# A decoder layer on one core: cross attention with one score pass, transposed exponentials and other PSUM banks

## What is computed

```python
Q = (q @ W_q.T + b_q).reshape(b, -1, NH, HD).transpose(0, 2, 1, 3)   # q: layernorm(x); NH = 16, HD = 32
K = (k @ W_k.T + b_k).reshape(b, -1, NH, HD).transpose(0, 2, 1, 3)   # k = v = context
V = (v @ W_v.T + b_v).reshape(b, -1, NH, HD).transpose(0, 2, 1, 3)
scores = jnp.einsum('bhqd,bhkd->bhqk', Q, K) / math.sqrt(HD)
scores = jnp.where(causal, -jnp.inf, scores)
scores = jnp.where(padding_mask[:, None, None, :], -jnp.inf, scores)
attn = jax.nn.softmax(scores, axis=-1)
out = jnp.einsum('bhqk,bhkd->bhqd', attn, V)
return out.transpose(0, 2, 1, 3).reshape(b, -1, H) @ W_o.T + b_o
```

## Time and profile before

| what | value |
|---|---|
| median of 3 runs | 4943.44 us (4933.94 to 4956.82) |
| the profiled execution, its own time | 4941.54 us |
| its span, first to last instruction | 4939.4 us |
| granted PE clock over the span | 0.919 |
| PE, DVE, ACT, POOL busy | 88%, 62%, 30%, 21% |

### The profile page before, as it was taken

The page is one execution under the profiler, slowest core; times in us unless marked ns, Lnnn a source line. Parts: engine busy times, 40 slices in busy tenths (PEclk is TensorE's granted clock), DMA queues, the critical chain, the costliest instruction groups (busy, mean ns, idle before and its releaser), DMA issues. The chain is left out here.

```text
span 4939.4 us, 62871 instructions
## 1 busy us (share of the span) xinstructions
PE 4366.1 (88%) x23000; PEld 2976.2 (60%) x23000; DVE 3085.8 (62%) x6572; ACT 1487.3 (30%) x2991; POOL 1046.1 (21%) x631
## 2 busy tenths in 40 slices
PE   7999999987989898986789779779888969999999
PEld 5667677755666666663544444454364447777777
DVE  5888888854888888886543344245234356666664
ACT  3433343323333333331134124214213411111111
POOL 1333333330444444444000000100100000000000
PEclk8999999998999999998877988889888879999999
DMA  2011111002111111111321321232132130000000
GB/s 97 35 38 36 37 38 38 33 15 87 36 46 40 40 36 46 40 37 53 129 78 33 119 82 48 96 101 60 57 116 68 39 105 26 31 30 26 30 26 22
DMA packets 146922, 265.55 MB, mean 54 GB/s; under 512 B 27188, under 2 KB 33336, under 8 KB 146616
## 3 DMA queue, kind: packets, MB, share of 16 engines
q1 hardware_dynamic: 144568, 261.27, 16.0%
q10 hardware_dynamic: 2048, 0.27, 0.0%
HBM read 164.58 MB, written 88.08 MB: 51 GB/s over the span
## 5 line engine op out<-in xcount | busy, mean ns | idle before, releaser
L1721 DVE TENSOR_REDUCE xa_mx<-xa_s 128x1 f32<-128x1024 f32 (+7 forms) x512 | 371.4, 746 | 343.7 <-PE xa_s L1795 336.1
L1623 ACT ACTIVATE xa_src<-xa_gen 128x512 f32<-128x512 f32 (+3 forms) x768 | 357.4, 491 | 547.4 <-PE xa_gen L1815 396.5
L1812 PE MATMUL xa_gen<-xa_qa,xa_ka 98*128 98x512 f32 (+3 forms) x768 | 351.6, 487 | 84.0 <-ACT xa_src L1623 52.4
L72 PE MATMUL ff_wb<-ff_w_hi,ff_st_hi 128*128 128x512 f32 x768 | 322.8, 420 | 17.1 <-DVE ff_parts L2308 11.1
L1572 POOL TENSOR_TENSOR xa_kq<-xa_kq 128x512 f32<-128x512 f32 x32 | 40.8, 1274 | 1374.8 <-DVE xa_kq L1727 1374.8
L1794 PE MATMUL xa_s<-xa_ka,xa_qa 97*128 97x512 f32 (+3 forms) x768 | 255.1, 398 | 78.5 <-DVE xa_mx L1721 55.8
L1812 PEld LDWEIGHTS xa_gen<-xa_qa,xa_ka 98*128 98x128 f32 x768 | 167.9, 222 | 251.0 <-issue 121.8
L73 PE MATMUL ff_wb<-ff_w_hi,ff_st_lo 128*128 128x512 f32 x768 | 310.2, 404 | 0.0
L74 PE MATMUL ff_wb<-ff_w_lo,ff_st_hi 128*128 128x512 f32 x768 | 309.4, 403 | 0.0
L1203 PE MATMUL mb_ib<-mb_wc,mb_yT 128*128 128x512 f32 x512 | 268.0, 672 | 1.8 <-DVE mb_y L974 1.0
L1203 PE MATMUL mf_ib<-mf_wc,mf_yT 128*128 128x512 f32 x512 | 249.6, 633 | 1.8 <-DVE mf_y L974 1.0
(11 more groups left out here) (513 smaller groups left out, 11395.6 us busy)
## 6 DMA issues: line engine op xcount, KB each, us to landing
xa_qa<-xa_q_dram SPq DMA_DIRECT2D x384, 64.0 KB, 2.0
xa_ka<-xa_k_dram SPq DMA_DIRECT2D x384, 64.0 KB, 2.0
xa_q_dram<-xa_kq SPq DMA_DIRECT2D x32, 512.0 KB, 2.8
xa_k_dram<-xa_kq SPq DMA_DIRECT2D x32, 512.0 KB, 2.8
mf_xg<-in_x_dram SPq DMA_DIRECT2D x16, 512.0 KB, 5.2
turned_dram<-mf_xt_hi SPq DMA_DIRECT2D x16, 512.0 KB, 2.6
turned_dram<-mf_xt_lo SPq DMA_DIRECT2D x16, 512.0 KB, 4.0
part_dram<-mf_hb SPq DMA_DIRECT2D x32, 256.0 KB, 2.0
```

Of the source, the lines that this page charges most:

```text
L72: nc.tensor.matmul(out, w_hi, x_hi, start=first, stop=False)
L1623: a_.activation(pe_x[:, s % 2, hh, 0:w], gen["p2", g, s, hh][:, 0:w], ACT.Exp, scale=XSCALE)\
L1721: v_.tensor_reduce(mx[:, g % 2, i, hh:hh + 1], s1[g, hh, i][:, 0:(i + 1) * P], AX.X, ALU.max)\
L1812: last = mm(ps[:, 0:n], ka[sl][0:ROW_MAX + 1, j * P:(j + 1) * P], qa[sl][0:ROW_MAX + 1, a:a + n], start=True, stop=not diagonal)
```

## The change

Scores are made once, with queries on the partitions. `W_q` and `b_q` are multiplied by `-XSCALE`, so the scores come negated and DVE takes a minimum (L1749), which is then the bias of the exponential: ACT computes `exp(-s + min)` from the same PSUM tile, up to 1024 columns wide, with the row sums in its accumulator (`accum_out`). PE transposes the exponentials in blocks of 128x128, up to four to a bank (`packs`, L1848), ACT and DVE copy the packs in turn to `pT`, and `weigh` uses them (L1864), now 128 queries at a time. The matmuls with ones, the second score pass, the row of maxima with its copies and DMAs are gone. DVE takes one reciprocal of 16 columns for a half, PE spreads it over partitions (`spread`, L1873), DVE copies that and multiplies. `gen` has three banks, the score tensors are handed out as four single banks or two pairs (`ScoreBanks`), `acc` has one. `ka` of slots 4 to 7 lies in `st_hi`, so group 1 is loaded when the projections are done. The order is one step for each query tile: the transposes and the weighing of the tile before stand between the four scores of this one.

```diff
+def packs(i):
+    if i == 0:
+        return [[(hh, 0) for hh in range(HG)]]
+    if i == 1:
+        return [[(hh, j) for hh in (a, a + 1) for j in range(2)] for a in (0, 2)]
+    out = []
     for hh in range(HG):
+        for a in range(0, i + 1, QT):
+            out.append([(hh, j) for j in range(a, min(i + 1, a + QT))])
     return out
...
+    def by_vector(i, k):
+        return k % 2 == 1 or i == 0
...
+        def loads(g):
+            for half in range(2):
+                for h in range(g * HG, (g + 1) * HG):
+                    yield "load", (h, "q", half)
+                    yield "load", (h, "k", half)
...
+            for n in range(len(TILES) + 1):
+                now, last = TILES[n] if n < len(TILES) else None, TILES[n - 1] if n else None
...
+                if scale:
+                    yield "scale", scale.pop()
+                yield from turns(0)
+                yield from turns(1)
+                yield from one("score", 0)
+                yield from turns(2)
+                yield from one("exp", 0)
+                yield from one("score", 1)
+                yield from turns(3)
+                yield from one("exp", 1)
+                yield from one("score", 2)
+                for _ in range(2):
+                    if todo and n > 0:
+                        yield todo.pop(0)
+                done = last and last[1] % QT == QT - 1
+                if done:
+                    yield "recip", (last[0], last[1] // QT)
+                if last:
+                    yield "av", last
+                if done:
+                    yield "spread", (last[0], last[1] // QT)
+                    scale.append((last[0], last[1] // QT))
+                yield from one("exp", 2)
+                yield from one("score", 3)
+                yield from one("exp", 3)
+                if now and now[1] == NT - 1 and now[0] + 2 < NHG:
+                    yield from loads(now[0] + 2)
+                if not todo and n == 4:
+                    yield from loads(1)
+                if now and now[0] == NHG - 1 and now[1] > QT + 1:
+                    yield "o", now[1] - QT - 2
...
-        gen = Banks(ctx, nc, tag + "gen", 2, gen)
-        s1 = Banks(ctx, nc, tag + "s1", 2, s1, 2 * BANK)
-        acc = Banks(ctx, nc, tag + "acc", 2, acc)
+        gen = Banks(ctx, nc, tag + "gen", 3, gen)
+        s1 = ScoreBanks(ctx, nc, tag + "s1", s1)
+        acc = Banks(ctx, nc, tag + "acc", 1, acc)
...
+                    a_.activation(pq[:, hh, 0:w], s1[g, i, hh][:, 0:w], ACT.Exp, scale=-1.0, bias=mn[:, i % 2, hh:hh + 1],
+                                  accum_out=sums[:, i // QT, i % QT, hh:hh + 1]).then_inc(p_ready.sem, 1)
...
+                    a_.activation(pT[:, k, 0:w], gen["turn", g, i, k][:, 0:w], ACT.Copy).then_inc(pta_ready.sem, 1)
...
+                    v_.tensor_reduce(mn[:, i % 2, hh:hh + 1], s1[g, i, hh][:, 0:(i + 1) * P], AX.X, ALU.min).then_inc(mx_ready.sem, 1)
...
+                    v_.tensor_copy(pT[:, k, 0:w], gen["turn", g, i, k][:, 0:w]).then_inc(ptv_ready.sem, 1)
...
+                    v_.tensor_copy(os[g][:, b, :], gen["spread", g, b][:]).then_inc(sp_ready.sem, 1)
+                    dve.wait_ge(sp_ready.sem, sp_ready.at(it, NQB * g + b))
+                    v_.tensor_tensor(os[g][:, b, :], acc["o", g, b][:], os[g][:, b, :], ALU.mult).then_inc(head_ready.sem, 1)
...
+                def turn(g, i, k):
+                    pe.wait_ge(p_ready.sem, p_ready.at(it, score_at(g, i, PACK[i][k][-1][0])))
+                    ps = gen.open(pe, it, ("turn", g, i, k))
+                    for n, (hh, j) in enumerate(PACK[i][k]):
+                        last = tr(ps[:, n * P:(n + 1) * P], pq[:, hh, j * P:(j + 1) * P], ident[:])
+                    last.then_inc(turn_full.sem, 1)
...
+                    for j in range(i + 1):
                         for hh in range(HG):
+                            k, a = at[hh, j]
+                            last = mm(ps[hh * XD:(hh + 1) * XD, c:c + P], vv[:, j, g * HG + hh, :], pT[:, k, a:a + P],
+                                      start=j == 0, stop=j == i, skip_group_check=True)
```

376 lines of the change are left out of this document (171 added, 205 removed).

## The result

| | before | after |
|---|---|---|
| median | 4946.74 us (4 runs, 4933.94 to 4956.82) | 4681.28 us (4 runs, 4674.54 to 4683.56) |
| ratio | | 0.9462, 95% interval 0.9437 to 0.9487 |
| span of the profiled execution | 4939.4 us | 4681.5 us |
| clock over the span | 0.919 | 0.950 |

The kernel is 5.4% faster: -265 us by the medians, -258 us by the spans. The forecast was 4785 us, that is -156. The sign and the range (4600 to 4915) held; the gain was 1.7 times the forecast one.

A forecast was written before the change was run, and what follows sets the result against it. It took PE to set the pace before and the chain of waits after: 4 x 62.3 + 22 = 271 us a batch, -136, tail and start -20, from 4941.5 to 4785 us, range 4600 to 4915.

The forecast's parts named there:

- The line of waits: Cross attention groups: each step's instructions wait in one chain through PE, DVE and ACT; 55 us a group.
- Rival 1: Cross attention groups: looser chain, little over the busiest engine, 47 us a group, 4540 us in all; chance 0.14.
- 2 to 4: Groups: clock at lower level, 5036 us (0.13); clock 0.70, 4877 (0.20 with rival 5); group 1's loads late, 4805 (0.05).
- rival 5: Wide steps: fourth score also waits for its bank, behind an exponential; 83 us more, 4868; chance 0.20 shared with clock 0.70.
- changes of the array: Weighing in each step: switching PE to parts of 32 columns and back, 0.3 us a step, 57.4 us a group.
- The clock: Cross attention groups: clock 0.84, 32% of the time at the lower level, raising a group from 57.4 to 62.3 us.
- Its 39.4 us in eight waits: Row of maxima through DRAM: DMA wait that goes whole, 39.4 us over four batches, 20 of them group 0's first score.
- The 44.5 us for keys: Group 0's first pass in the kernel before: waits for loads of keys, 44.5 us.
- rival 2: Cross attention groups: clock stays at the lower level, 76 us a group, 5036 us in all; chance 0.13.
- Group 0: First group of each batch: its steps carry the ten projections left over, +22 us a batch.
- Sources and tail: Tail and start of a batch: smaller reciprocal, outputs reordered, four single source banks; 5 us a batch, -20 us.
- The loads: Group 1's loads wait for all projections but are covered by group 0's later steps; cost 0, else up to 5 us a batch.

The follow-up runs named there:

- the run with loads head by head: Kernel after, with loads issued head by head, front and back, instead of the fronts of all four heads first: 4711.41 us, ratio 0.9512.
- The pause put into the mixed order: Against the mixed order: VectorE repeats tile 2's first minimum six more times in each of groups 1 to 3; 4640.79 us, ratio 0.9389.
- the mixed order: Kernel after, with weighing ahead of the fourth score and two heads' transposes early in tiles 5 to 7, fourth score first in tiles 0 to 4: 4587.24 us.
- the run with pairs: Kernel after, with a pair of banks for every score tile and source, none single: 4750.32 us, ratio 0.9591.
- two orders that gained 40 us and nothing clear by themselves: Each against the kernel after: fourth score ahead of the weighing, 4641.06 us; transposes two heads behind their exponential, 4665.89 us.

## Why the prediction was right in sign and short in size

**The line of waits** was the right bound. The walk gave 55 us a group at the upper clock, and 55.2 was measured. Six changes of order or of banks moved the attention part between 922 and 1130 us while DVE and ACT stayed within 604 to 622 and 586 to 602 us of busy time. Rival 1 (a group at little over its busiest engine) didn't come, nor did 2 to 4. What rival 5 names is there, 36.4 us of PE's waits of score matmuls for exponentials, but mostly beside the line: in the step shown the weighing ahead of the fourth score ends at 2945.58, later than that score's bank is free (2944.50, the end of exponential 1).

**The sum of a group** was 62.3 us: 55 walked, 2.4 for changes of the array, 4.9 for the clock. The mean of the twelve groups 1 to 3 is 57.5: 55.2 for the steps, 0.7 for the outputs in group 3, and 1.6 for the clock. That the mean comes so near to the 57.4 which the prediction had at the upper clock is chance. The 2.4 us, 38 us over 16 groups, were read from two starts of the kernel before and do not show in the steps of this one.

**The clock was the term that failed most.** I took 0.84 for the groups, 32% of the time at the lower level, because PE would be busy with less of them, from the windows with less PE work in the earlier trace rows. It was 0.96 to 0.99 over the four stretches. By the clock's own record 58 us of the 1020.8 were at the lower level, all of them in groups 1 to 3, 8% of these groups. The twelve take 689.6 us and would take 670.4 at 1.00 throughout (eight of 55.2; four of 57.2, as group 3 has it in the run with loads head by head), so the clock cost 19 us in all, where the forecast had 16 x 4.9 = 78. In the kernel before 324 of the 1242.2 us were at the lower level (0.84 to 0.90). What its 324 us cost in time isn't shown, so how much of the gain is the clock's is open. The rows of before had a better sign in another place. The mean clock of a window says how often the clock fell in it, not what made it fall:

```profile
2894.30:2897.70 3.40, 1.04 (x8) 0.60 (x8) 1.27 (x2) 1.06 (x2) 0.00 (x0) 1.00 0.86 252
2897.70:2921.60 23.90, 14.39 (x55) 7.88 (x55) 4.54 (x11) 4.35 (x8) 0.00 (x0) 0.50 0.44 118
```

These two windows of the kernel before are the turn of the maxima and the wait for their row: PE waits with 1.0 us busy of 3.4 at clock 1.00, then goes on waiting for DMAs (4.76 us for the row up to 2901.42, then 2.03 and 3.76 us for keys up to 2910.78), and the clock is 0.50 for 23.9 us with PE busy for 14.4 of them. In the kernel after a fall looks like this (batch 1, start of group 1):

```profile
2841.60:2845.00 3.40, 1.96 (x24) 1.38 (x15) 2.70 (x6) 1.21 (x5) 0.00 (x0) 1.00 0.46 118
2845.00:2855.30 10.30, 9.73 (x59) 7.29 (x59) 5.32 (x11) 5.74 (x18) 0.00 (x0) 0.50 0.49 130
2855.30:2893.60 38.30, 29.26 (x386) 22.38 (x384) 25.68 (x38) 25.94 (x55) 0.00 (x0) 1.00 0.09 29
```

It too stands behind a stretch with PE little busy, 1.96 of 3.4 us. But here PE is nearly full as soon as its work takes twice as long (9.73 of 10.3), and the clock comes back; then PE is busy with 29.3 of 38.3 us, less than in any group of the earlier trace rows, and the clock holds 1.00. The prediction read the waits themselves too large and in part in the wrong place. Its 39.4 us in eight waits are four, one a batch, each listed for the weight load and for the matmul:

```profile
PEld xa_gen L1812 <- DMA xa_qa<-xa_rows: 20.3, 4, 5.3
PE xa_gen L1812 <- DMA xa_qa<-xa_rows: 19.1, 4, 5.0
```

The 44.5 us for keys are likewise 21.5 us in eight waits, and they lie in group 1's first pass, behind the row of maxima, not in group 0's. (The score and attention part is five windows of the earlier trace rows, not six.) None of this entered the sum. With these waits went the low stretches of over 20 us that lay around them, which argues that removing them was worth more than their own 19 and 21 us. The pause put into the mixed order shows that a long pause of PE brings a low stretch; that it explains each fall of the kernel before is argued from such rows, not tested.

**Transposes.** By the rule of the Trainium skill ("TensorE: Matmul & The Clock Gate", Part 4: PE-mode transpose) that I weighed, a transpose doesn't count for the clock as other work does. These traces show 335 us of transposes (L1848) amid windows at 0.91 to 1.00, and the mixed order holds 1.00 over whole stretches of 230.3 us, in which they are 40% of PE's busy time (82 of 203 us). The row was the better guide, and rival 2 had less for it than its 0.13.

**Group 0** cost 73.8 us at clock 1.00, 18.6 over a group's 55.2; the forecast had 22, 4 x 3.4 = 14 us too dear. Its windows had no low stretch, and its steps with two projections each took 9.3 to 10.7 us.

**A term was left out**: what lies ahead of the first exponential and behind the last. The last tile's transposes and its weighing have nothing beside them but the outputs: the mean stretch of 255.2 less 73.8 and three times 57.5 is 9.0 us a batch, 36 us.

**Sources and tail**: -29.9 and -7.0 measured for the -20 forecast. The tail brought 7, not 20; the sources brought the rest, by their four single banks, which I had named in half a sentence, as the run with pairs shows. **The loads** were hidden, as forecast, at cost 0.

The account: -156 forecast, -59 for the clock (19 instead of 78), -38 for the changes of the array, +3 for the walk (16 x 0.2), +8 for the outputs in group 3, -14 for group 0, +36 for the ends, -17 for sources and tail, which is -237. The last -21 are a matter of windows: I closed the stretches of the earlier trace rows 5 us ahead of the end of the last weighing and compared them with a sum that runs to it. Together that is the -258 of the spans.

## What to carry to other kernels

When no engine is full in a stretch, walk one step of the line of waits with durations from the trace. It gave each step of the kernel as built within 0.6 us and named the instruction to move. For changes of order it was less sure: of five, it forecast -75 for -40, -121 for -15, a gain for a loss of 84, +120 for +120 (in part by the clock) and 4590 to 4610 for 4587. What frees a bank belongs on the line: a third bank for the turned blocks was worth 120 us. A move that shortens one step shows its true worth only when the steps beside it are measured too: two orders that gained 40 us and nothing clear by themselves gave 94 us together, part of it by the clock. A long pause of PE costs more than itself, since low stretches follow it; the mean clock of a window can't be carried to another kernel. And look whether a list of waits counts one wait for two engines.

## What the runs showed of the hardware

- A pause of PE of some 3 us in full work (1.3 us busy in its first 3.4) was followed 11 times in 12 by 3.4 to 6.8 us at the lower clock, and each such fall cost about 1.8 us beyond the pause. A shorter one, the same in twelve groups (1.8 us busy of 3.4), was followed by a fall in 8 of them.
- PE busy with 29.3 of 38.3 us, in pieces with short waits between, kept the clock at 1.00. So did stretches of 230.3 us with 40% of PE's busy time in fp32 transposes.
- The read-out of ACT's accumulator has a record of 0.19 to 0.21 us, but the next instruction starts 0.09 us behind its start, and leaving out 512 of them took 43 us off ACT's busy time.
